# The first layer's convolution on TensorE: folded weights, four shifted products, chunks interleaved

## The reference, cut to what matters

```python
xz = x @ W_in_o + b_in_o                       # x: layer-normed tokens, (2048, 128)
x_proj, z_proj = (xz[..., :D_INNER], xz[..., D_INNER:])   # D_INNER = 256
xz2 = x_proj @ W_in_i
xm, zm = (xz2[..., :D_INNER], xz2[..., D_INNER:])
xc = silu(causal_depthwise_conv(xm, conv_w, conv_b))      # four taps per channel
dbl = xc @ W_xp
dt = dbl[..., :DT_RANK]
Bm = dbl[..., DT_RANK:DT_RANK + D_STATE]                  # D_STATE = 16
Cm = dbl[..., DT_RANK + D_STATE:]
delta = jax.nn.softplus(dt @ W_dt + b_dt)
y = selective_scan(delta, Bm, Cm, xc, A) + D_skip * xc
y = y * silu(zm)
out_i = y @ W_out_i
out = out_i * jax.nn.sigmoid(z_proj)
return out @ W_out_o + b_out_o
```

## Time and profile before

| | |
|---|---|
| median of 3 runs | 1906.49 us (1905.56 to 1908.88) |
| the profiled execution | 1910.42 us |
| its span | 1908.7 us |
| TensorE busy | 1514.1 us, 79% |
| VectorE busy | 1273.4 us, 67% |
| ScalarE busy | 883.9 us, 46% |
| GpSimd busy | 431.8 us, 23% |
| first scan starts | 103.18 us |

### The profile page before, as it was taken

How to read it: one execution, slowest core, us unless ns; L and a number is a source line. 1 busy time by engine, 2 the same in 40 slices (tenths; PEclk the granted TensorE clock), 3 DMA queues, 4 the chain that set the end, 5 groups by cost and what they waited for, 6 DMA issues and landing times.

```text
span 1908.7 us, 28354 instructions
## 1 busy us (share of the span) xinstructions
PE 1514.1 (79%) x8083; PEld 654.4 (34%) x8084; DVE 1273.4 (67%) x2879; ACT 883.9 (46%) x1705; POOL 431.8 (23%) x291
## 2 busy tenths in 40 slices
PE   6656565439999999999407903999999999859999
PEld 3222222222333333332305802233333333246665
DVE  8499998458888888882431115888888888234444
ACT  3733232011777777777102301277777777712111
POOL 5379898020010011110151061010000111100000
PEclk9879899765999999999658956599999999959999
DMA  3112122032111111110511123211111111000001
GB/s 74 36 55 77 67 76 90 0 103 49 39 43 47 50 39 38 51 30 9 169 41 50 47 47 101 51 51 40 38 51 38 40 48 38 1 17 17 17 16 30
DMA packets 60626, 91.78 MB, mean 48 GB/s; under 512 B 13017, under 2 KB 41121, under 8 KB 60545
## 3 DMA queue, kind: packets, MB, share of 16 engines
q1 hardware_dynamic: 58514, 86.79, 15.8%
q0 software_dynamic: 2048, 4.20, 0.9%
HBM read 74.63 MB, written 16.32 MB: 48 GB/s over the span
## 4 chain that ended last, share of the span: by engine, by line
PE 67%; DVE 20%; ACT 4%; POOL 4%; issue 3%; DMA 2%; SPq 1%; DVEq 0%; POOLq 0%; ACTq 0%
PE psum_a L961 17%; PE psum_a L943 14%; PE psum_b L931 12%; DVE arena L599 5%; DVE arena L573 4%; PE psum_a L1599 3%; PE psum_b L1599 3%; PE psum_a L358 2%; PE psum_b L1608 2%; ACT psum_a L497 2%; DVE extra L1132 2%; PE psum_b L358 2%; PE psum_a L1608 2%; POOL expert_inputs L1349 2%; POOL arena L1355 2%
## 5 line engine op out<-in xcount | busy, mean ns | idle before, releaser
L1071 ACT ACTIVATE arena<-psum_a 128x512 f32<-128x512 f32 (+3 forms) x1280 | 595.0, 537 | 197.9 <-PE psum_a L943 105.7
L1132 DVE TENSOR_REDUCE extra<-psum_b 128x1 f32<-128x512 f32 x768 | 486.9, 683 | 75.4 <-PE psum_b L931 73.6
L931 PE MATMUL psum_b<-arena 72*128 72x512 bf16 (+3 forms) x1280 | 424.6, 370 | 52.2 <-DMA arena<-k_parts 50.5
L943 PE MATMUL psum_a<-arena 75*128 75x512 bf16 (+3 forms) x1280 | 417.3, 354 | 3.7 <-ACT arena L1071 3.7
L961 PE MATMUL psum_a<-arena,extra 128*32 128x512 f32 x2560 | 345.1, 611 | 1.8 <-ACT arena L1071 1.4
L1129 DVE CUSTOM_DVE_ANT_0 extra<-psum_b,mask_q 128x512 bf16<-128x512 f32 (+3 forms) x512 | 224.6, 487 | 77.9 <-PE psum_b L931 65.0
L943 PEld LDWEIGHTS psum_a<-arena 75*128 75x128 bf16 x1280 | 118.8, 98 | 353.6 <-ACT arena L1071 285.7
L334 POOL TENSOR_TENSOR arena<-arena,extra 128x1024 f32<-128x1024 f32 x48 | 170.7, 3569 | 42.0 <-DVE arena L599 29.7
L931 PEld LDWEIGHTS psum_b<-arena 72*128 72x128 bf16 x1280 | 119.1, 100 | 171.7 <-DMA arena<-k_parts 50.9
L877 POOL TENSOR_TENSOR arena<-arena 128x512 f32<-128x512 f32 x64 | 81.6, 1276 | 416.4 <-ACT arena L1062 282.4
L1062 ACT ACTIVATE arena<-psum_a 128x512 f32<-128x512 f32 x128 | 76.4, 597 | 95.2 <-PE psum_a L961 95.2
(11 more groups left out here) (288 smaller groups left out, 1674.2 us busy)
## 6 DMA issues: line engine op xcount, KB each, us to landing
arena<-q_parts SPq DMA_DIRECT2D x192, 96.0 KB
arena<-k_parts SPq DMA_DIRECT2D x192, 96.0 KB
extra<-c_rows SPq DMA_DIRECT2D x32, 512.0 KB, 3.5
arena<-in_L_ffn_fc_w_dram SPq DMA_DIRECT2D x32, 256.0 KB, 5.8
k_parts<-arena SPq DMA_DIRECT2D x10, 512.0 KB, 5.5
q_parts<-arena SPq DMA_DIRECT2D x6, 512.0 KB, 4.9
...
```

What stands on the lines that cost most here:

```text
L931: m = e.matmul(ps[:, at:at + width], s.mq[0:ROWS, b, i * P:(i + 1) * P], s.mk[0:ROWS, b, c * CW:c * CW + width], start=True, stop=True)
L943: m = e.matmul(score_bank(p)[:, at:at + width], s.ek[0:ROWS + 3, b, j * P:(j + 1) * P], s.eq[0:ROWS + 3, b, (c + 1) * CW - width:(c + 1) * ...
L1071: m = e.activation(probabilities(s, b, kind, quad, k, width), score_bank(p)[:, at:at + width], ACT.Exp)
L1132: m = e.tensor_reduce(s.mpart[:, i, c:c + 1], ps[:, at:at + length], AX.X, ALU.max)
```

## The change

The convolution leaves VectorE. Since the taps act on each channel by itself, W_xz's columns can be scaled by a tap and the convolution becomes four products that are added up in PSUM, over four views of xT shifted by one token each. xT gets three zero columns in front (PAD). The scaled weights come from one product per half: the turned fold of the weights times four diagonal matrices, which VectorE makes from the identity (L579 of the changed kernel, eight TENSOR_SCALAR). The convolution's bias is b_xz times the sums of taps, in four columns: the first three tokens see fewer taps, so ScalarE reads them as single columns. Silu is applied when the conv piece is read, so xc needs no pass of its own.

One list, PIECE_ORDER, now sets the order on TensorE and on ScalarE. Chunk c's bc and delta stand ahead of chunk c + 2's conv pieces. The z half of the folded weights (w_z), the z products and the gate products stand behind all chunks, and ScalarE reads w_z, z and the gates behind the last Ln. ScalarE's second read of delta with Abs goes; VectorE forms the negative of the absolute value from delta instead (L601). conv_w moves to the early loads, and the third load of c_rows waits for the last piece, since xT lies where it writes.

```diff
         x_tok = slot(0)
-        xn, xT = slot(1), slot(2)
+        xn = slot(1)
+        PAD = 3
+        xT = extra[:, HALF * 2:HALF * 2 + PAD + T]
...
-        sp_z = [half_slots(1, 3, c) for c in range(NC)]
+        sp_z = [half_slots(2, 3, c) for c in range(NC)]
         sp_w = [half_slots(15, 17, c) for c in range(NC)]
...
+        diag_ready, bias_ready, sp_a_ready = sem("diag_ready"), sem("bias_ready"), sem("sp_a_ready")
-        PIECES = gate_part(NC, 0)
+        PIECE_ORDER = ["in_turn", "xz_turned", ("xT", 0), "b_xz", ("w_conv", 0), ("w_conv", 1), ("xT", 1),
+                       ("conv", 0, 0), ("conv", 0, 1), "xp_turn", ("xT", 2), "w_delta", ("conv", 1, 0), ("conv", 1, 1)]
+        for c in range(NC):
+            PIECE_ORDER += [("bc", c), ("delta", c, 0), ("delta", c, 1)]
+            if c + 3 < NC:
+                PIECE_ORDER.append(("xT", c + 3))
+            if c + 2 < NC:
+                PIECE_ORDER += [("conv", c + 2, 0), ("conv", c + 2, 1)]
+        PIECE_ORDER.append("w_z")
+        PIECE_ORDER += [(what, c, m) for what in ("z", "gate") for c in range(NC) for m in range(NM)]
+        PIECE = {x: n for n, x in enumerate(PIECE_ORDER)}
+        PIECES = len(PIECE_ORDER)
...
                 (b_in, a["L0_attn_b_in_o"].rearrange("(m p) -> p m", p=P)),
+                (conv_w, a["L0_attn_conv_w"].rearrange("(m p) k -> p m k", p=P)),
             ]
             for dst, src in early:
...
             e.wait_ge(c_stored, 16)
-            e.wait_ge(conv_done, NM * NC)
+            e.wait_ge(piece_filled, PIECE["conv", NC - 1, NM - 1] + 1)
             for step in range(STEPS):
+                if step == 2:
+                    e.wait_ge(piece_filled, PIECES)
                 if step >= NCB:
                     e.wait_ge(hc1_done, step - NCB + 1)
                 h, n = step // NS, step % NS
...
+            def turn(n, blocks):
+                ps = piece(n)
+                for t, block in enumerate(blocks):
+                    i = e.transpose(ps[:, t * P:(t + 1) * P], block, ident[:, :])
                 i.then_inc(piece_filled, 1)
+
+            def chunk(c, shift=PAD):
+                return xT[:, c * CW + shift:(c + 1) * CW + shift]
+
+            for n, what in enumerate(PIECE_ORDER):
+                kind = what if isinstance(what, str) else what[0]
+                c, m = (what + (0,))[1:3] if kind != what else (0, 0)
...
+                elif kind == "xz_turned":
+                    e.wait_ge(piece_freed, PIECE["in_turn"] + 1)
+                    ps = piece(n)
+                    for k in range(NM):
+                        i = product(ps[:, k * P:(k + 1) * P], [w_in_i[:, j, k * P:(k + 1) * P] for j in range(NM)],
+                                    [w_turned[:, j * P:(j + 1) * P] for j in range(NM)])
+                    i.then_inc(piece_filled, 1)
...
+                elif kind == "w_conv":
+                    e.wait_ge(piece_freed, PIECE["xz_turned"] + 1)
+                    e.wait_ge(diag_ready, NM)
+                    product(piece(n), [w_xz[:, c * P:(c + 1) * P]], [diag[:, c, :, :]]).then_inc(piece_filled, 1)
+                elif kind == "xT":
+                    e.wait_ge(xn_ready, c + 1)
+                    turn(n, [xn[:, (4 * c + t) * P:(4 * c + t + 1) * P] for t in range(4)])
+                elif kind == "conv":
+                    e.wait_ge(consts_ready, PAD_READY)
+                    e.wait_ge(piece_freed, max(PIECE["w_conv", m], PIECE["xT", c]) + 1)
+                    product(piece(n), [w_conv[:, m, k * P:(k + 1) * P] for k in range(PAD + 1)],
+                            [chunk(c, k) for k in range(PAD + 1)]).then_inc(piece_filled, 1)
...
+                elif kind == "w_z":
+                    product(piece(n)[:, 0:DI], [w_turned[:, k * P:(k + 1) * P] for k in range(NM)], [w_in_i[:, k, DI:2 * DI] for k in range(NM)]).then_inc(piece_filled, 1)
+                elif kind == "bc":
+                    e.wait_ge(xc_ready, c + 1)
+                    product(piece(n)[0:2 * NS, :], [w_xp[:, k, P:P + 2 * NS] for k in range(NM)],
+                            [xc[:, k, c * CW:(c + 1) * CW] for k in range(NM)]).then_inc(piece_filled, 1)
+                elif kind == "delta":
+                    e.wait_ge(piece_freed, PIECE["w_delta"] + 1)
+                    product(piece(n), [w_delta[:, k, m * P:(m + 1) * P] for k in range(NM)],
+                            [xc[:, k, c * CW:(c + 1) * CW] for k in range(NM)]).then_inc(piece_filled, 1)
+                elif kind == "z":
+                    e.wait_ge(piece_freed, PIECE["w_z"] + 1)
+                    product(piece(n), [w_xz[:, DI + m * P:DI + (m + 1) * P]], [chunk(c)]).then_inc(piece_filled, 1)
+                else:
+                    product(piece(n), [w_in_o[:, DI + m * P:DI + (m + 1) * P]], [chunk(c)]).then_inc(piece_filled, 1)
...
+            for n, what in enumerate(PIECE_ORDER[:PIECE["w_z"]]):
+                kind = what if isinstance(what, str) else what[0]
+                c, m = (what + (0,))[1:3] if kind != what else (0, 0)
                 cols = slice(c * CW, (c + 1) * CW)
+                if kind == "in_turn":
+                    std(0, slice(0, 4))
+                    read(n, w_turned[:, 0:DI], ACT.Copy, width=DI)
...
+                elif kind == "w_conv":
+                    read(n, w_conv[:, c, :], ACT.Copy)
+                    if c == 1:
+                        std(1, slice(4, NT))
+                elif kind == "xT":
+                    read(n, xT[:, PAD + c * CW:PAD + (c + 1) * CW], ACT.Copy)
...
+                elif kind == "conv":
+                    e.wait_ge(bias_ready, 1)
+                    e.wait_ge(piece_filled, n + 1)
+                    if c == 0:
+                        for t in range(PAD):
+                            e.activation(xc[:, m, t:t + 1], bank(n)[:, t:t + 1], ACT.Silu, bias=conv_bias[:, m, t:t + 1])
+                    first = PAD if c == 0 else 0
+                    i = e.activation(xc[:, m, c * CW + first:(c + 1) * CW], bank(n)[:, first:CW], ACT.Silu, bias=conv_bias[:, m, PAD:PAD + 1])
+                    i.then_inc(piece_freed, 1)
+                    if m == NM - 1:
+                        e.wait_ge(piece_freed, n + 1)
+                        e.sem_inc(xc_ready, 1)
+                elif kind == "bc":
+                    read(n, bc32[:, cols], ACT.Copy, m=32)
+                else:
+                    read(n, delta[:, m, cols], ACT.Identity, b_dt[:, m:m + 1])
             e.activation(a_neg[:, :, :], a_neg[:, :, :], ACT.Exp)
             for c in range(NC):
+                e.wait_ge(sp_a_ready, c + 1)
+                e.activation(sp_z[c], sp_z[c], ACT.Exp).then_inc(sp_z_ready, 1)
             for c in range(NC):
                 e.wait_ge(sp_w_ready, c + 1)
                 e.activation(sp_w[c], sp_w[c], ACT.Ln).then_inc(sp_l_ready, 1)
+            read(PIECE["w_z"], w_xz[:, DI:2 * DI], ACT.Copy, width=DI)
             for c in range(NC):
                 for m in range(NM):
+                    read(PIECE["z", c, m], gate_in[:, m, c * CW:(c + 1) * CW], ACT.Silu, b_xz[:, NM + m:NM + m + 1])
+            for c in range(NC):
+                for m in range(NM):
+                    read(PIECE["gate", c, m], gate_out[m][:, c * CW:(c + 1) * CW], ACT.Sigmoid, b_in[:, 2 + m:3 + m])
...
             variances(0, slice(0, 4))
+            e.wait_ge(early_loaded, 16 * EARLY_LOADS)
+            e.wait_ge(consts_ready, IDENT_READY)
+            for m in range(NM):
+                for k in range(PAD + 1):
+                    i = e.tensor_scalar(diag[:, m, k, :], ident[:, :], conv_w[:, m, k:k + 1], None, ALU.mult)
+                i.then_inc(diag_ready, 1)
             normalize(0, slice(0, 4))
+            def biases():
+                e.wait_ge(mamba_weights_loaded, 16 * MAMBA_LOADS)
+                e.wait_ge(piece_freed, PIECE["b_xz"] + 1)
+                last = conv_b
+                for t in range(PAD + 1):
+                    now = conv_bias[:, :, t]
+                    dve_link(e, e.tensor_tensor(now, b_xz[:, 0:NM], conv_w[:, :, PAD - t], ALU.mult))
+                    i = e.tensor_tensor(now, now, last, ALU.add)
+                    if t < PAD:
+                        dve_link(e, i)
+                    last = now
+                i.then_inc(bias_ready, 1)
+
             variances(1, slice(4, NT))
+            biases()
             normalize(1, slice(4, NT))
-
-            e.wait_ge(consts_ready, PAD_READY)
-            e.wait_ge(mamba_weights_loaded, 16 * MAMBA_LOADS)
             for c in range(NC):
-                cols = slice(c * CW, (c + 1) * CW)
-                for m in range(NM):
-                    e.wait_ge(piece_freed, first_part(c, XM + m) + 1)
-                    taps = [xm[:, m, c * CW + k:c * CW + k + CW] for k in range(4)]
-                    dve_link(e, e.tensor_scalar(conv[:, m, cols], taps[0], conv_w[:, m, 0:1], conv_b[:, m:m + 1], ALU.mult, ALU.add))
-                    for k in range(1, 4):
```

(8 more changed lines are left out.)

115 lines of the change are left out of this document (32 added, 83 removed).

## The result

The changed kernel takes 1934.55 us in the median of four runs (1931.29 to 1940.02), the kernel before 1907.68 in four: ratio 1.014 (95%: 1.0101 to 1.018). In five later runs it was 1934.93 against 1910.6, 1.0126 (1.0106 to 1.0146). The profiled execution took 1931.34 (span 1929.6), 20.9 us of span more than before. The forecast was 1927, and for 8 in 10 it gave 1914 to 1935.

The account below looks back on a forecast made before the run. The prediction took the first scan's start (103.18), set by the stretches ahead of it, as what matters. Terms 14.2 + 1.9 + 0.4 + 3.9 = 20.4 us on 1906.49 gave 1927; own range 1922 to 1932, 8 in 10 1914 to 1935.

Parts of the forecast that it names:

- (c): Rival for the tail: TensorE's clock stays low through z and gates, +32 us, 1938; chance 0.08.
- The diagonals and the selects: Front: GpSimd's selects hold VectorE's eight diagonals, two of nearly 3.8 us; first chunk at 23.2, against 8.25 before.
- (a): Rival for the front: VectorE's stream keeps the port lock, everything 4 us earlier, +16.4, 1923; chance 0.13.
- (b): Rival for the front: diagonals not held at all, conv starts 11.5 us earlier, +8.9, 1915; chance 0.12.
- The chunks: Conv (0,0) to last delta: TensorE needs 47.9 us, so Exp's table loads near 88.4, 14.2 us later.
- (d): Rival for the chunks: an accumulated product takes one record, not two; not slower, -4 to -1, 1904; chance 0.04.
- Softplus: Exp's table to last Ln: GpSimd's late add holds VectorE's first TENSOR_SCALAR, 1.9 us lost; port contention adds 0.4.
- The tail: Last Ln to first scan: w_z's read, then z and gates partly at low clock; 19.9 instead of 16.0, cost 3.9.
- What follows the scan: First scan onward: nothing edited, so the end gains or loses what the first scan does; scan stage length unchanged.

Follow-up runs that it names:

- x10: Changed kernel with w_z read before softplus, GpSimd's three selects after the normalisations, and its output-bias add behind the second split; 1912.06 us, ratio 1.0009.
- x2: Changed kernel with GpSimd's three large selects waiting until all tokens are normalised; 1920.82 us, ratio 1.0069.
- x4: Changed kernel with w_z read before softplus and GpSimd's three large selects waiting for the normalisations; 1918.88 us, ratio 1.0036.
- x3: Changed kernel with three of the four taps of every conv piece left out, only the time being meant; 1915.65 us, ratio 1.0028.
- x5: Changed kernel with all conv pieces ordered ahead of all bc and delta pieces; ratio 1.0123.
- x7: Kernel before, convolution kept on VectorE, with z's products and reads late and the next chunk's Silu before the delta reads; 1899.14 us, ratio 0.9951.
- x1: Changed kernel with w_z read right behind the last delta, ahead of Exp, not behind the last Ln; 1931.19 us, ratio 1.0121.

## Why the prediction was right

The mechanism and the sum held: +20.4 forecast, +19.66 at the first scan, +20.9 in the span. The medians rose by more, 26.9 and 24.3 us. The forecast's ratio of 1.0107 lies at the lower end of both intervals (1.0101 to 1.018, 1.0106 to 1.0146), the median of 1934.55 outside the forecast's own range of 1922 to 1932 and 0.5 us inside the wider one, whose upper end had been moved towards (c), a rival that did not occur. Step by step:

- **The diagonals and the selects.** Two of them were to lie nearly 3.8 us under a select, with room for two between the selects: they lay there 3.85 each, from 8.15 and 12.12, and one passed in between. Wrong was the start. I had conv_w land after the first select began; it landed at 7.2, four diagonals had started ahead of the held one at 8.15, and the first chunk came 2.5 us earlier than forecast. Rival (a), a VectorE stream that keeps the port, was refuted each time: the waiting select got in after one diagonal. Rival (b), no hold, exists once the selects wait: it put the first conv record at 23.1, and it came at 22.2 at the low rate (x10) and 18.2 at the high one (x2, x4).
- **The chunks.** 47.9 us forecast from the end of conv (0,0) to the last delta, 49.3 measured. From one bc to the next conv piece it is 5.38 (62.62 to 68.00) where I counted 5.16, and a conv piece is 3.48 (68.00 to 74.96, two of them) where I counted 3.44: 0.9 and 0.3 over all. x3 and x5 show that this stretch is TensorE's and that the order does not change its length. Rival (d), one record for a product, is out: a piece of four products is x8.
- **Softplus.** 1.9 + 0.4 forecast, 2.8 measured. The instruction held was not the first TENSOR_SCALAR, which got through in 0.96, but the two-input one behind it (5.41). By the Trainium skill (SBUF — State Buffer, "Who interferes with whom") an instruction of VectorE's with two SBUF inputs contends with a GpSimd instruction that reads SBUF, and the add reads the tokens there; the 5.41 agrees, and so does GpSimd's 2.09 beside VectorE's last minus-and-min at 86.71, where that step took it 1.15 in the chunk before. In x4 and x7 the same add held the first TENSOR_SCALAR instead (5.03 and 4.09), as the prediction had it: which of the two was held went by when the add began (89.69, behind the start of the TENSOR_SCALAR at 89.20; ahead of it, at 76.51 and 63.84, in x4 and x7).
- **The tail.** 3.9 forecast, 4.35 measured, and by the path named: 16 us of standing, 0.50 of the clock, first eight records 5.86, the last sigmoid, B's spread, VectorE waiting 4.37. x1 took the read away and the tail was 16.0 again. Rival (c), a clock that stays low, did not occur: it was at 1.00 from 108 to 124.
- **What follows the scan** is unchanged (232.3 against 231.7), up to the first product behind the scans, and the span less first scan is 1805.5 and 1806.8: in these two executions the first scan's delay is the end's.

Errors of -3.0, +1.3, +0.5 and +0.4 us cancelled in part, which was luck. The profiled execution was also one of the two fastest, and the median lies 3 us above it, while the one of the kernel before lay 3.9 above its median of then: the 5 to 7 us by which the medians differ more than the first scans have no term in the forecast, and no run shows where they lie.

What the change lost, by the runs: of the 19.7 us at the first scan 9.2 go when GpSimd's selects make way (and 4.0 more where TensorE has the high rate), 4.3 with one read, 4.3 with GpSimd's add. Of these the add's hold was there before too, though shorter. With all three mends and the low rate, as in the kernel before, the first scan is at 106.03 against 103.18. These are ways to win the time back and not shares of one sum: leaving out three taps won back 19.8 by itself, and the mends give the change a front that the kernel before hasn't. And what the interleaving was to give could be had with the convolution left on VectorE: 10 us earlier, with z late and the next Silu early.
